# A two-layer transformer block on Trainium2: linear attention steps reordered, and more of the cross attention's preparation among them

## The reference, cut to what matters

```python
def _L1_attn_ref(H, ...):                       # linear attention
    q, k, v = split(H @ W_qkv.T + b_qkv)        # 16 heads of 16
    q, k = elu(q) + 1, elu(k) + 1
    kv = einsum('bhnd,bhnv->bhdv', k, v); k1 = k.sum(axis=2)
    out = (q @ kv) / clip(q . k1, 1e-06)
    out = out.reshape(B, N, D)                  # heads not moved back: a regrouping
    out = layernorm(out @ W_proj.T + b_proj) * gamma + beta
    return out + H

def _L1_xattn_ref(x, y, ...):                   # y: context, 1601 x 192 per image
    q, k, v = x @ Wq + bq, y @ Wk + bk, y @ Wv + bv   # 8 heads of 32
    return softmax(q @ k.T / sqrt(32)) @ v @ Wo + bo

x = _layernorm(x + _L1_attn_ref(x, ...))
x = _layernorm(x + _L1_xattn_ref(x, ctx_768, ...))
```

## Time and profile before

| | |
|---|---|
| runs, median (lowest to highest) | 2840.47 us (2838.47 to 2840.93) |
| profiled execution | 2848.74 us, span 2847.4 us |
| granted TensorE clock, mean over the span | 0.876 |
| linear attention | 1193.3 to 1398.2 us of the span |
| lead-in of the cross attention | 1398.2 to 1477.2 |

### The profile page before, as it was taken

One profiled execution on the slowest core, in us unless ns is written; L12 is line 12 of the kernel. 1 busy time (PEld: TensorE's weight loads), 2 busy tenths in 40 slices (PEclk: granted clock), 3 DMA queues, 4 the chain that ended last, 5 costly groups with the idle time before them and its releaser, 6 DMA issues. The chain is left out here.

```text
span 2847.4 us, 41664 instructions
## 1 busy us (share of the span) xinstructions
PE 2229.3 (78%) x15694; PEld 1432.6 (50%) x15694; DVE 1674.0 (59%) x3413; ACT 1182.0 (42%) x2185; POOL 566.6 (20%) x489
## 2 busy tenths in 40 slices
PE   6993589896408999287589999995888697788678
PEld 3552157573306888144235555653555444455534
DVE  4666965568763333466556565643777642677663
ACT  2222844345232333132225555553665442566442
POOL 2110000001363554401200000001222141322052
PEclk9996789998658999589689999997899898899999
DMA  3005000100360111323311111102000001000000
GB/s 109 1 1 155 14 1 1 45 1 1 96 215 26 46 46 38 108 65 79 102 48 36 24 36 24 24 13 88 1 1 1 11 1 59 1 1 1 36 12 23
DMA packets 75074, 113.30 MB, mean 40 GB/s; under 512 B 22916, under 2 KB 59744, under 8 KB 74208
## 3 DMA queue, kind: packets, MB, share of 16 engines
q1 hardware_dynamic: 71808, 102.24, 12.0%
q0 software_dynamic: 3072, 8.39, 0.9%
HBM read 85.38 MB, written 31.20 MB: 41 GB/s over the span
## 5 line engine op out<-in xcount | busy, mean ns | idle before, releaser
L2479 DVE TENSOR_REDUCE xa_max<-psum 128x1 f32<-128x1024 f32 (+1 forms) x256 | 248.8, 988 | 144.7 <-PE psum L2382 144.1
L2575 ACT ACTIVATE xa_work<-psum 128x1024 f32<-128x1024 f32 (+1 forms) x208 | 212.9, 1024 | 202.1 <-PE psum L2405 200.5
L2420 PE MATMUL psum<-xa_work,xa_values 128*33 128x128 f32 (+1 forms) x3328 | 232.1, 284 | 0.0
L2420 PEld LDWEIGHTS psum<-xa_work,xa_values 128*33 128x33 f32 (+1 forms) x3328 | 172.9, 114 | 78.9 <-issue 73.7
L2774 PE MATMUL psum<-wqkv_l,x_hl_l 128*128 128x512 bf16 x576 | 146.1, 401 | 60.6 <-POOL x_hl_l L3034 32.4
L3140 PE MATMUL psum<-h_ch_f,w_f 128*128 128x512 bf16 (+1 forms) x576 | 139.3, 400 | 32.1 <-DVE h_ch_f L3200 9.5
L1645 DVE TENSOR_SCALAR moe_raw<-psum,tile_b 128x256 f32<-128x256 f32 x184 | 78.3, 474 | 139.3 <-PE psum L1487 138.2
L2405 PE MATMUL psum<-xa_query_rows,xa_key_rows 98*128 98x512 bf16 (+1 forms) x416 | 131.5, 399 | 8.4 <-ACT xa_work L2575 7.7
L1741 POOL TENSOR_TENSOR x_ch<-moe_raw,x_ch 128x512 bf16<-128x512 f32 x92 | 105.5, 1158 | 149.9 <-ACT x_ch L1701 147.8
L1487 PE MATMUL psum<-moe_rows,moe_w 128*128 128x256 bf16 x1104 | 132.9, 279 | 3.0 <-POOL moe_rows L1737 3.0
L2382 PE MATMUL psum<-xa_key_rows,xa_query_rows 96*128 96x512 bf16 (+1 forms) x512 | 129.4, 348 | 6.7 <-DVE xa_max L2479 3.0
(11 more groups left out here) (439 smaller groups left out, 4832.2 us busy)
## 6 DMA issues: line engine op xcount, KB each, us to landing
xa_key_rows<-cross_keys SPq DMA_DIRECT2D x48, 200.1 KB, 3.5
moe_raw<-in_moe_w SPq DMA_DIRECT2D x16, 512.0 KB, 5.2
x_ch<-in_moe_w SPq DMA_DIRECT2D x16, 512.0 KB, 4.8
moe_rows<-slots_in SPq DMA_DIRECT2D x23, 256.0 KB, 2.8
slots_out<-moe_rows SPq DMA_DIRECT2D x23, 256.0 KB, 2.1
ctx_f<-in_ctxT SPq DMA_DIRECT2D x2, 2401.5 KB, 21.5
cross_keys<-xa_k_hl SPq DMA_DIRECT2D x6, 800.5 KB, 3.7
xa_query_rows<-cross_queries SPq DMA_DIRECT2D x48, 64.0 KB, 3.5
```

What stands on the lines that cost most here:

```text
L2420: ins = pe.matmul(total.ap[a * LANE:a * LANE + VC, c:c + PIECE], t["v"][b][0:rows, kt, first + a, :], exps[0:rows, a, c:c + PIECE], start= ...
L2479: v.tensor_reduce(t["maxes"][n % 2][:, qt * HU + a, part:part + 1], u.wide[:, 0:c1 - c0], AX.X, ALU.max).then_inc(*u.free)
L2575: act.activation(t["exps"][k % EXPS][0:rows], u.wide[0:rows].rearrange("p (m q) -> p m q", q=T), ACT.Exp, scale=1.0 / float(np.sqrt(np.flo ...
```

## The change

The order of the linear attention is written anew. The steps `inputs`, `read` and `project` are cut into single products (`q`, `kv`, `read`, `project` with their tile numbers). The norm of a projection becomes `spread` (statistics), `root` (ACT) and `scale` (with gamma on DVE and beta on POOL), that of the close becomes `close` (addition and statistics), `root_last` and `finish`. The plan of image b interleaves pieces of images b+1, b, b-1 and b-2, and at 41 places marked `gap` it puts one or two steps of a side list of 48. That list now holds the parts of all four contexts, with those of image b+1 placed before the last value steps of image b, for which high parts have two buffers. `x_split`, `queries` and `asked` of images 0 to 2 stand in the main order, and the query weights are split with the others. In the cross attention only image 3's are left, after its keys and values. The row loads of the first three units stand at its start, and the first exponentials wait also for the store of image 3's queries. On ACT the Exp of a kv step goes ahead of the copy. Signals are raised once per group in the norms. The regrouped channels have one buffer (`la_oc`) in place of two, and key parts share memory with the float weights. The arithmetic is the same.

The new order around image 2 reads, side steps between bars: `state.1 q.2.0 q.2.1 | context.1 | kv.2.0 project.0.0-3 kv.2.1 | keys | spread.0 kv.2.2 | keys | kv.2.3 | rows | root.0 read.1.0 scale.0 read.1.1 read.1.2 close.0 read.1.3 | keys || keys | regroup.1 | rows | root_last.0 state.2 q.3.0 finish.0 q.3.1 | value | kv.3.0 channels.0 project.1.0-3 kv.3.1 ...`, and at the end: `... read.3.3 | rows || keys | regroup.3 | keys | root_last.2 finish.2 | rows | channels.2 | value | x_split.2 | value | project.3.0-3 | value | spread.3 queries.2.0 queries.2.1 asked.2 | value | root.3 | parts.3 | scale.3 | value | close.3 | value | root_last.3 | value | finish.3 | context.3 | channels.3`. Between `regroup.2` and `project.2` stand two values, `state.3`, `finish.1` and `channels.1`.

```diff
 def linear_plan():
-    plan = [("inputs", 0)]
+    gap = [("gap",)]
+    inputs = lambda b: [("q", b, c) for c in range(HALVES)] + [("kv", b, n) for n in range(TPB)] if 0 <= b < B else []
...
+    steps = inputs(0)[:2] + gap + inputs(0)[2:4] + gap + inputs(0)[4:] + gap
     for b in range(B):
-        plan += [("inputs", b + 1)] if b + 1 < B else []
-        plan += [("state", b), ("read", b)]
-        plan += [("project", b - 1)] if b else []
-        plan += [("regroup", b)]
-        plan += [("channels", b - 3)] if b > 2 else []
-        plan += [("close", b - 2)] if b > 1 else []
-    plan += [("channels", B - 3), ("close", B - 2), ("project", B - 1), ("close", B - 1), ("channels", B - 2), ("channels", B - 1)]
-    side = [("weights",)] + flat([[("parts", b), ("context", b)] + key_steps(b) + value_steps(b) for b in range(AHEAD)])
-    return plan[:2] + mingle(plan[2:], side)
+        new, old, older = inputs(b + 1), b - 1, b - 2
+        steps += [("state", b)] + new[:1] + only(older, "finish") + new[1:2] + gap + new[2:3] + only(older, "channels") + project(old)
+        steps += new[3:4] + gap + split(older) + only(old, "spread") + new[4:5] + gap + new[5:] + queries(older) + gap + only(old, "root")
+        for n in range(TPB):
+            steps += [("read", b, n)] + (only(old, "scale") if n == 0 else only(old, "close") if n == 2 else [])
+        steps += gap + gap + [("regroup", b)] + gap + only(old, "root_last")
+    last, old = B - 1, B - 2
+    steps += only(old, "finish") + gap + only(old, "channels") + gap + split(old) + gap + project(last) + gap + only(last, "spread")
+    steps += queries(old) + gap + only(last, "root") + gap + only(last, "scale") + gap + only(last, "close") + gap
+    steps += only(last, "root_last") + gap + only(last, "finish") + gap + only(last, "channels")
+    side = [("weights",)]
+    for b in range(AHEAD):
+        values = value_steps(b)
+        side += ([("parts", b)] if b == 0 else []) + [("context", b)] + key_steps(b) + values[:4] + [("parts", b + 1)] + values[4:]
+    side.append(("context", AHEAD))
...
 def cross_plan():
-    rest = asked(2) + asked(3) + flat([key_steps(b) + value_steps(b) for b in range(AHEAD, B)])
-    plan = asked(0) + [("parts", B - 1), ("context", B - 1)] + asked(1) + mingle(rest, maxima[:lead])
+    rest = key_steps(AHEAD) + [("x_split", AHEAD)] + value_steps(AHEAD) + [("queries", AHEAD, c) for c in range(HALVES)] + [("asked", AHEAD)]
+    plan = rest[:2] + mingle(maxima[:lead], rest[2:])
...
 def cross_sp(m, s, t, use, plan):
-    sp.dma_start(t["w_f"][:], dram["xa_q"].rearrange("(h p) o -> p h o", h=2)).then_inc(*s.w_loaded.up(16))
-    context_sp(m, s, t, B - 1)
+    for u in range(3):
+        load(u)
...
 def cross_act(m, s, t, use, plan):
             else:
                 for o in range(HALVES):
                     act.wait_ge(*keys_stored(s, o)(16))
+                act.wait_ge(*s.q_stored(16))
                 act.wait_ge(*use["value", B - 1, KT - 1].full)
```

More of the change, by code:

```diff
@@ L1767 @@
+    side.append(("context", AHEAD))
+    gaps, done, plan = steps.count(("gap",)), 0, []
+    for step in steps:
+        if step != ("gap",):
+            plan.append(step)
+        else:
+            gaps -= 1
+            upto = done + -(-(len(side) - done) // (gaps + 1))
+            plan += side[done:upto]
+            done = upto
+    return plan
 AHEAD = B - 1
@@ L1794, in linear_attention @@
         plan = linear_plan()
-        norms = [p for p in plan if p[0] in ("project", "close")]
-        nth = {p: n + 1 for n, p in enumerate(norms)}
+        nth = {p: n + 1 for n, p in enumerate(p for p in plan if p[0] in ("root", "root_last"))}
         steps = []
         for step in plan:
[L1799 to L1807, removed]
+            if step[0] in ("q", "kv", "state", "read", "project"):
+                steps.append(step)
+            elif step[0] in ("regroup", "channels"):
+                steps += [step + (h,) for h in range(HALVES)]
@@ L1808, in linear_attention @@
         use = m.banks(steps, (4, 5, 6, 7))
-        use.update(m.banks([p for p in plan if p[0] in ("keys", "value")], (0, 2)))
+        use.update(m.banks([p for p in plan if p[0] in ("keys", "value", "queries")], (0, 2)))
         linear_sp(m, s, t, use, plan)
@@ L1830, in linear_sp @@
         kind, b = step[0], step[-1]
-        if kind == "regroup":
-            oc = t["o_ch"][b % 2]
+        if kind == "asked":
+            for c in range(HALVES):
+                sp.wait_ge(*use["queries", b, c].done)
+            asked_sp(m, t["q_hl"][:], b).then_inc(*s.q_stored.up(16))
+        elif kind == "regroup":
+            oc = t["o_ch"]
             sp.wait_ge(*use["regroup", b, 1].done)
@@ L2004, in linear_dve @@
+            ins.then_inc(*u.free)
+        elif kind == "project":
+            n, u = step[2], use[step]
+            v.wait_ge(*u.full)
+            v.tensor_tensor(projected(m, b)[:, n // 2, n % 2, :], u.ap[:, 0:D], m.row("la_bproj"), ALU.add).then_inc(*u.free)
+        elif kind == "spread":
             for n in range(TPB):
                 v.wait_ge(*use["project", b, n].done)
-                v.bn_stats(m.stats[:, TPB * b + n, :], tiles[n]).then_inc(*s.v_step.up())
-            v.wait_ge(*s.v_step.now())
@@ L2097, in prepare_pe @@
     pe, kind = m.nc.tensor, step[0]
-    if kind == "keys":
+    if kind == "queries":
+        b, c = step[1:]
+        u = use[step]
+        pe.wait_ge(*s.x_low(b - first + 1))
+        pe.wait_ge(*u.empty)
+        for h in range(HALVES):
+            for n, (x, w) in enumerate(PASSES):
+                ins = pe.matmul(u.ap, t["wq"][:, w, h, c * P:(c + 1) * P], t["x_hl"][:, x, h, :],
+                                start=(h, n) == (0, 0), stop=(h, n) == (1, 2))
+        ins.then_inc(*u.fill)
+    elif kind == "keys":
         b, o, c0 = step[1:]
@@ L2170, in prepare_act, with split_pool @@
         act.activation(t["k_hl"][o][:, 0, c0:c1], u.wide[:, 0:c1 - c0], ACT.Identity, bias=m.col("xa_bk", o)).then_inc(*s.in_high.up())
+def split_pool(m, s, t, use, b, first=0):
+    g = m.nc.gpsimd
+    g.wait_ge(*s.x_high(b - first + 1))
+    if b > first:
+        for c in range(HALVES):
+            g.wait_ge(*use["queries", b - 1, c].full)
+    g.tensor_tensor(t["x_hl"][:, 1], m.x_ch[:, :, b * T:(b + 1) * T], t["x_hl"][:, 0], ALU.subtract).then_inc(*s.x_low.up())
 def context_pool(m, s, t, n):
     g = m.nc.gpsimd
-    both = t["c_both"][CTX_B:P, 0:S2]
+    both = t["c_both"][n % 2][CTX_B:P, 0:S2]
     g.wait_ge(*s.c_split(2 * n + 2))
@@ L2202, in cross_plan @@
 def cross_plan():
-    def asked(b):
-        return [("x_split", b)] + [("queries", b, c) for c in range(HALVES)] + [("asked", b)]
     maxima = []
```

426 lines of the change are left out of this document (202 added, 224 removed).

## The result

The changed kernel takes 2849.51 us (median of 7 runs, 2847.94 to 2851.84). The kernel before takes 2840.47 beside it (7 runs). The ratio is 1.0029, 95% interval 1.0017 to 1.0040, so it is **slower, by 5 to 11 us**, where the prediction had 11 faster. Run again among the experiments, on a chip where the kernel before took 2848.74, it gave 1.0022 (1.0002 to 1.0042); its ten executions there lie between 2842.46 and 2864.23, far wider apart than the seven of the first measurement, and the one that was profiled is among the longest (2863.07).

The account below looks back on a forecast made before the run. Neither VectorE (59% busy) nor TensorE (78%) is full; waits in fixed orders bound both stretches. Stage +7 - 20 + 28 + 3 = +18, lead-in -29, together -11: 2848.7 becomes 2838, median 2829; range 2800 to 2850.

Parts of the forecast that it names:

- rival C: Four projections: TensorE idles through each trip, its clock falls, queued work runs slower; adds some 24, giving 2853; chance 0.15.
- The lead-in, minus 29: Start of cross attention: work leaves it, so exponentials start 52 us in, not 81; ends minus 26 and minus 36.
- The stage gains work, plus 7: Linear stage: VectorE gets six query steps, a low part and a weight part, +7.0, on the path.
- the tail's plus 3: After the last projection: GpSimd's addition stands behind its context 3 part and VectorE waits; plus 3 (0 to 6).
- Waits that go: Linear stage: VectorE's waits for keys, q products, values and square roots shrink; minus 20, ends minus 3 and minus 33.
- The wait that comes, plus 28: Four projections: VectorE waits for the regroup's round trip through memory, 32.6 less today's 5.0; ends minus 5 and plus 46.
- A: Whole kernel as forecast: lead-in shrinks, round trips give back over half; 2815 to 2842; chance 0.50.
- B: Linear stage: round trip hidden, stage doesn't lengthen; 2811, or 2796; sign: regrouped-tile waits under 10 in all; chance 0.25.
- D: Three of GpSimd's moved instructions each hold a VectorE instruction of two SBUF inputs for 3.0; -11 + 9, 2838; chance 0.10.

Follow-up runs that it names:

- Version 6: Old order of the kernel before with all the moved work, GpSimd's parts of the next context ahead of an image's last values: 0.9895 of the kernel before.
- runs 10 and 11: Version 6 with ten buffer zeroings ahead of VectorE's first attention step: 0.9907; version 6 with TensorE's three pauses filled by matmuls: 0.9891 of the kernel before.
- run 9: The kernel before with matmuls filling TensorE's three 2.56 us pauses in the exponentials' stretch: 0.9941 of the kernel before.
- Run 2: Changed kernel with an image's four readings together, regroup straight behind them, scaling and closing after the regroup: 0.9973 of the kernel before.
- Run 1: Changed kernel whose projection multiplies a slice of the weights, so TensorE does not wait for the regrouped tiles: 0.9963 of the kernel before.
- run 7: Changed kernel with unused matmuls in TensorE's idle time at the turn and ahead of the projections of images 2 and 3: 1.0020 of the kernel before.
- runs 2 and 3: Run 2 has its line; the other is the changed kernel with each projection moved behind the next image's keys, values and the queries: 0.9962 of the kernel before.

## Why the prediction was wrong

It said faster, and the kernel is slower. The median of 2849.5 lies just inside the range of 2800 to 2850 only because half of rival C had been let into it, which was luck.

**The lead-in, minus 29: right.** The exponentials start 52.8 us in (forecast 52), and the subtraction of unit 0 ends at 43.1 (forecast 43.4). TensorE's first scores start 6.8 us in, and the first maximum on VectorE 8.4 (forecast 7 to 8). ScalarE's last wait ahead of them is the one named, for the store of image 3's queries, 3.9 us.

**The stage gains work, plus 7, with the tail's plus 3: right, near enough.** VectorE's busy time rose by 9.3, and its wait for GpSimd's addition by 2.1 (4.0 after 1.9). GpSimd explains the excess over 7: it held two instructions for 2.9 us each (below), where the earlier trace rows showed one, for 3.0. Version 6, the moved work in the old order, has a stage 10.0 longer than before.

**The step that failed is "Waits that go", minus 20** (its terms add up to 19.2). They came to minus 2: keys -3.1 (forecast -9.5), values +3.7 (-3.7), q products -0.3 (-3), roots -2.4 (-3). "Single key steps between main steps should hide about half" was argued from the order alone. Version 6, with coarse steps, has the same 15.9 for keys, and 17.6 and 17.7 in runs 10 and 11, while the kernel before has 17.3 in run 9. So even the 3.1 may be chance. In the key step VectorE waits for ScalarE's share of that same step, and finer main steps around it did not shorten that.

**What the sum lacked** is a term for TensorE. I took VectorE for the late engine in most steps, and so counted its waits for TensorE's state (7.6) and kv products (4.8) at nothing, and the wait for ScalarE's part of the queries (2.5) too: 14.9 us in all. I never asked what the readings' new neighbours do to TensorE, which stands at the turn until the last reading, nor what is queued behind it. Run 2, which puts the readings together and the work from among them into the trip, shortens the stage by 18, and the waits of the projection, the state and the turn with it.

**The wait that comes, plus 28: right in kind, too long in size.** It measured 16.6 (21.6 - 5.0). For images 0 to 3 VectorE waited 4.2, 3.0, 8.7 and 5.6 us (forecast 5.4, 3.9, 12.0 and 11.3), since it met other waits inside the trips, 3.94 and 1.91 in the rows of image 2's above. The trips were not shorter: from the turn to the end of the projection on VectorE 20.5 to 23.1 us passed, where the forecast had 18.8 from rows at the upper clock. Run 1 puts the worth of all this at 18 of the stage.

Together: 9.3 busy, 16.6 projection, -2.1, 14.9, and 3.5 for GpSimd's addition and the copies is 42; the stage grew by 41. That says where VectorE waited, and not what each wait would give if it went. The runs show that the order is the cause, and that the trip with its low clock is 18 of it. The rest they don't take apart: run 2's stage is still 12.9 longer than version 6's, 3.0 of it busy time, 6.8 the addition behind GpSimd, 4.6 kv, 4.3 the projection and 2.4 the state, against 5.4 for queries and 2.9 for roots that version 6 waits more.

**The rivals.** A's lead-in was right, its stage was not. B is out: the waits for the regrouped tiles are over 10. C named the sign, the bound (over 29) and the size (2853, measured 2849.5), and its mark was there (stage over 235, a granted clock of 0.59 to 0.69 behind each trip). Its mechanism is at most a part: run 7 raised the clock behind the turns and got no time for it, and behind the trips, where only one of four was helped, the rows above allow it some 7 us of C's 24. It got the number right by chance, in the main. D's three held instructions were two, for one before. With the pauses filled in both kernels the change costs 1.0004 over 0.9941, 0.6%, or 18 us. Why filling gives the kernel before 17 us and the changed kernel only 5, when the stretches in their profiles gain 14 and 13, is not settled; only one execution of each was profiled.

## What to carry to other kernels

When steps are set apart in a hand-written order of several engines, cost the order once for each engine: for each step that one engine must wait for, ask what stands behind it in that engine's queue, and who runs dry meanwhile. Here one edit that put four readings together, and the work from among them into the trip, gave as much as leaving out the whole trip to DRAM. And the moved work itself paid in the old order (29 us of lead-in gained for 10 of stage, 14 us of the whole time with the pauses filled in both). A pause of TensorE is priced by what the clock does after it as well, so a version that wins in a stage next to such pauses should be measured with them filled too.

## What was not expected of the hardware

- A pause of 2.56 us in a TensorE that is else busy without a break was followed by the lower clock of 1.2 GHz for some 10 us ((1.00 - 0.63) / 0.50 x 14), though TensorE was busy for all of those 14. In another kernel the same pause was followed by 1.00, the upper clock. Eleven matmuls in each pause kept the clock up, 13 to 14 us for three pauses.
- Two edits that gave 18 and 12 us of the stage (runs 2 and 3) gave 15 together. That they undo the same loss in part fits this, and is not shown by a run of its own.
- GpSimd held VectorE twice in the changed kernel. An instruction that takes 0.42 us elsewhere took 3.33, and one of 1.23 took 4.14, each begun within 0.4 us of GpSimd's sum of context parts. From the timeline:

```profile
1210.86 3.23 POOL L2269 TENSOR_TENSOR xa_c_both<-xa_ctx_f,xa_c_both 64x1601 bf16<-64x1601 f32 x1 [19.45 <-ACT xa_c_both L2244]
...
1211.04 3.33 DVE L1996 SCALAR_TENSOR_TENSOR la_k<-la_kv,la_min 128x256 f32<-128x256 f32 x1 [1.35 <-ACT la_min L2090]
...
1421.48 3.44 POOL L2269 TENSOR_TENSOR xa_c_both<-xa_ctx_f,xa_c_both 64x1601 bf16<-64x1601 f32 x1 [16.60 <-ACT xa_c_both L2244]
...
1421.85 4.14 DVE L2034 TENSOR_TENSOR x_ch<-x_ch,rows 128x1024 f32<-128x1024 f32 x1
```

VectorE's first ends 0.28 us after GpSimd's (1214.37 and 1214.09), its second 1.07 after (1425.99 and 1424.92), about its own time. The Trainium skill (SBUF — State Buffer, "SBUF: two separate sides") says that whichever of two such instructions starts first has the shared ports until it is done, and the other waits. The trace agrees, by these numbers, and once the other way round:

```profile
1344.06 4.28 POOL L2269 TENSOR_TENSOR xa_c_both<-xa_ctx_f,xa_c_both 64x1601 bf16<-64x1601 f32 x1
```

Here VectorE's addition had begun 0.04 us before (1344.02, shown above) and took its usual 1.23, and GpSimd's sum took 4.28 in place of 3.2 to 3.4. A start that close does not decide by the profile's times, though: in version 6 GpSimd's beta begins at 1319.83, 0.10 us ahead of a low part on VectorE, and is itself the longer one, 4.12 us for 2.34, while VectorE's takes its usual 1.82.
